# First norm of the next pair in the second feed-forward, value buffers cleared by ACT between its key copies, coupling behind the third tile

## The reference, cut to what matters

```
x = x + attn_a(layernorm(x))   # local attention, 16 heads of 16, blocks of 32 tokens, softmax
x = x + ffn(layernorm(x))      # three cycles of a gated coupling
x = x + attn_b(layernorm(x))   # differential attention, 32 half heads over all 1024 tokens
x = x + ffn(layernorm(x))
```

```
def layernorm(x):  return (x - mean(x)) / sqrt(var(x) + 1e-5)
def attn_a(x):     q, k, v = x @ w_qkv.T + b_qkv; softmax(q k / 4) v in blocks of 32 tokens
def ffn(x):
    gf = global_net(mean over tokens of x)
    out = x
    for _ in range(3):
        tf = sigmoid(gelu(gelu(gelu(out@w1+b1)@w2+b2)@w3+b3)@w4+b4)
        coupling = 0.1 + range * (0.7*gf + 0.3*tf - 0.5) * 2
        out = out + coupling * twist(out)      # twist permutes quarters of the features
    return out
```

## Time and profile before

| | us |
|---|---|
| median of 3 runs | 8516.29 |
| lowest, highest | 8493.72, 8532.59 |
| the profiled execution's own time | 8488.95 |
| its span (first to last instruction) | 8484.5 |
| PE, DVE, ACT, POOL busy | 7651.8, 6965.3, 6290.1, 3252.0 |
| mean granted clock of PE, share of full | 0.959 |

### The profile page before, as it was taken

How to read it: one execution, slowest core, us unless ns; L and a number is a source line. 1 busy time by engine, 2 the same in 40 slices (tenths; PEclk the granted TensorE clock), 3 DMA queues, 4 the chain that set the end, 5 groups by cost and what they waited for, 6 DMA issues and landing times. The chain is left out here.

```text
span 8484.5 us, 166411 instructions
## 1 busy us (share of the span) xinstructions
PE 7651.8 (90%) x65584; PEld 2773.6 (33%) x65584; DVE 6965.3 (82%) x8955; ACT 6290.1 (74%) x11674; POOL 3252.0 (38%) x4567
## 2 busy tenths in 40 slices
PE   6899978999789997899988999889998899979999
PEld 3322343223432234322343223432234322343223
DVE  5899768997689976899768997689976899668996
ACT  3699756997569975699756997569975699656996
POOL 3244232442324423344233442334423344234441
PEclk9999989999899998999999999999999999989999
DMA  0100001000010000100001000010000100001000
GB/s 30 46 21 23 17 11 46 21 24 15 11 46 21 24 15 11 46 24 21 15 11 46 25 21 15 11 50 21 22 19 6 50 21 25 18 4 50 22 23 21
DMA packets 219176, 205.43 MB, mean 24 GB/s; under 512 B 108086, under 2 KB 143414, under 8 KB 218358
## 3 DMA queue, kind: packets, MB, share of 16 engines
q1 hardware_dynamic: 218364, 194.46, 8.0%
HBM read 123.83 MB, written 67.37 MB: 23 GB/s over the span
## 5 line engine op out<-in xcount | busy, mean ns | idle before, releaser
L1440 DVE TENSOR_REDUCE mfull<-ps 128x1 f32<-128x1024 f32 x4096 | 4707.9, 1217 | 328.6 <-PE ps L1362 327.7
L1515 ACT ACTIVATE work<-ps 128x512 f32<-128x512 f32 x8192 | 4405.8, 598 | 373.6 <-PE ps L1384 257.5
L1402 PE MATMUL ps<-work,vbuf 128*32 128x256 f32 x32768 | 2624.1, 392 | 119.5 <-ACT hh L1535 119.5
L1362 PE MATMUL ps<-kop,qop 48*128 48x512 bf16 x8192 | 2490.4, 385 | 47.8 <-DVE mfull L1440 24.3
L1384 PE MATMUL ps<-qop,kop 51*128 51x512 bf16 x8192 | 2488.8, 384 | 0.9 <-DMA qop<-mT 0.7
L1402 PEld LDWEIGHTS ps<-work,vbuf 128*32 128x32 f32 x32768 | 654.4, 108 | 1769.3 <-issue 968.2
L1384 PEld LDWEIGHTS ps<-qop,kop 51*128 51x128 bf16 x8192 | 481.6, 93 | 1641.3 <-ACT work L1515 1525.8
L1466 POOL CAST mpart<-mfull 128x16 bf16<-128x16 f32 x256 | 50.4, 197 | 2467.0 <-issue 2004.2
L251 POOL TENSOR_TENSOR rstd<-rstd,nhalf 128x8 f32<-128x8 f32 x64 | 109.3, 1707 | 1632.4 <-DVE rstd L245 1632.4
L1484 POOL TENSOR_TENSOR work<-work,none 128x16 f32<-128x16 f32 x224 | 650.3, 2903 | 18.8 <-POOL mpart L1470 1.5
L450 POOL TENSOR_TENSOR hh<-work,hmask 128x1024 f32<-128x1024 f32 x256 | 520.7, 2062 | 111.4 <-PE ps L382 79.0
(11 more groups left out here) (178 smaller groups left out, 8868.0 us busy)
## 6 DMA issues: line engine op xcount, KB each, us to landing
qop<-scratch SPq DMA_DIRECT2D x512, 64.0 KB
scratch<-work SPq DMA_DIRECT2D x32, 768.0 KB, 4.1
scratch<-hh SPq DMA_DIRECT2D x32, 768.0 KB, 3.6
kop<-scratch SPq DMA_DIRECT2D x256, 96.0 KB
vbuf<-in_x SPq DMA_DIRECT2D x9, 2048.0 KB, 8.3
qop<-scratch SPq DMA_DIRECT2D x512, 32.0 KB
kop<-scratch SPq DMA_DIRECT2D x256, 64.0 KB
qop<-mT SPq DMA_DIRECT2D x1024, 3.0 KB
```

Source lines behind the costliest of these rows:

```text
L1362: pe.matmul(ps[:, b + n, :], qop[r:r + KQ, s, i, t * P:(t + 1) * P], kop[r:r + KQ, s, i, half(n)], start=True, stop=True).then_inc(s_ms, 1)
L1402: mm = pe.matmul(ps[VW * i:VW * (i + 1), OB, cols], vp[:, b, t, (G * gl + i) // 2, :], prob[:, u % PS, i, cols], start=t == 0 and part == ...
L1440: v.tensor_reduce(mfull[:, m // CUT % 2, r // ROWS * G // 2 + i, to:to + 1], ps[:, b:b + NB, :].rearrange("p b n -> p (b n)"), AX.X, ALU.m ...
L1515: act.activation(prob[:, u % PS, hl, :], ps[:, EB[slot % len(EB)], :], ACT.Exp, scale=scale).then_inc(s_ex, 1)
```

## The change

`first_pair` normalises, turns and keeps all 16 tiles instead of 8, and POOL clears `work[:, 8N:12N]` and `low` in that block. The block n1 is gone from the loop, and `layernorm` loses the arguments that served it. In f2 (`following`), behind the last residual tile, DVE normalises tiles 8 to 15 of the next pair into `h`; PE turns them behind the four key pieces, into banks 0 to 3, once two of these pieces are kept; and ACT and DVE keep them. ACT clears the four pieces of buffer by copying a broadcast column of zeros (a new tile `zero`), one of 2048 elements ahead of each key copy. In f2 alone, `couple(1, 2)` and `couple(1, 3)` stand ahead of tiles 3 and 4 of sequence 0.

```diff
@@ first_pair
-                    for t in range(T):
+                    for t in range(TT):
                         v.tensor_scalar(h[:, t, :], xin[:, t, :], mv[:, t, 0:1], rstd[:, t:t + 1],
                                         ALU.subtract, ALU.mult).then_inc(s_h, 1)
+                @block.gpsimd
+                def _(pool):
+                    pool.memset(work[:, 8 * N:12 * N], 0.0)
+                    pool.memset(low[:, :], 0.0)
+
                 @block.tensor
                 def _(pe):
-                    for t in range(T):
+                    for t in range(TT):
                         norm_turned(pe, t, s_h, s_tp)
-                    pe.wait_ge(s_ln, C * NB)
+                    pe.wait_ge(s_ln, C * CH)
                     for k in range(len(KV)):
                         first_keys(pe, k, 2 * k, s_qk)
                 @block.scalar
                 def _(act):
-                    for n in range(NB):
+                    for n in range(CH):
+                        b, cols = chunk_of(n)
                         act.wait_ge(s_tp, 4 * (n + 1))
                         for c in range(C):
-                            act.copy(hT[:, 0, c, half(n)], ps[:, c * NB + n, :]).then_inc(s_ln, 1)
+                            act.copy(hT[:, b, c, cols], ps[:, 4 * b + c * NB + n % NB, :]).then_inc(s_ln, 1)
@@ ffn, tensor
                             first_keys(pe, k, 2 * k, s_nqk)
+                        pe.wait_ge(s_nqke, 2)
+                        for t in range(T, TT):
+                            pe.wait_ge(s_nh, t + 1)
+                            for c in range(C):
+                                at = (t % 4) * P
+                                mm = pe.transpose(ps[:, c * NB + t % T // 4, at:at + P], h[:, t, c * P:(c + 1) * P],
+                                                  ident[:, :])
+                            mm.then_inc(s_ntp, 1)
@@ ffn, scalar
                     if following:
                         act.wait_ge(s_y, CH)
+                        act.wait_ge(s_pre, len(COUPLED))
+                        act.wait_ge(s_rw, 16 * len(COUPLED) // NB)
                         for k in range(len(KV)):
+                            clear = (work[:, 8 * N:10 * N], work[:, 10 * N:12 * N], low[:, 0:2 * N],
+                                     low[:, 2 * N:4 * N])[k]
+                            act.copy(clear, zero[:, 0:1].to_broadcast([P, 2 * N]))
                             act.wait_ge(s_nqk, k + 1)
                             keep_first_keys(act, k, 2 * k, s_nqke)
+                        for n in range(NB):
+                            act.wait_ge(s_ntp, T + 4 * (n + 1))
+                            act.copy(hT[:, 1, 0, half(n)], ps[:, n, :])
@@ ffn, vector
-                    for t in range(T):
-                        if t == T - 1:
-                            couple(1, 2)
-                        add_twisted(0, t)
-                    couple(1, 3)
+                    at = (T - 1, T) if q is None else (3, 4)
+                    for t in range(T + 1):
+                        if t in at:
+                            couple(1, 2 + at.index(t))
+                        if t < T:
+                            add_twisted(0, t)
...
+                    if following:
+                        v.wait_ge(s_xo, TT)
+                        v.wait_ge(norm[2], PB)
+                        for t in range(T, TT):
+                            v.tensor_scalar(h[:, t, :], xin[:, t, :], mv[:, t, 0:1], rstd[:, t:t + 1],
+                                            ALU.subtract, ALU.mult).then_inc(s_nh, 1)
+                        for n in range(NB):
+                            v.wait_ge(s_ntp, T + 4 * (n + 1))
+                            v.tensor_copy(hT[:, 1, 1, half(n)], ps[:, NB + n, :])
@@ the loop
-            layernorm("n1", x=xin, later=True)
             local_attention(n2)
```

More of the change, by code:

```diff
@@ L107, in build @@
         none = sb("none", [P, DH // 2])
+        zero = sb("zero", [P, 1])
         hb4 = sb("hb4", [P, 1])
@@ L168, in _ @@
                 pool.memset(none[:, :], -1.0).then_inc(s_c, 1)
-                pool.wait_ge(s_c, 2)
+                pool.memset(zero[:, :], 0.0).then_inc(s_c, 1)
+                pool.wait_ge(s_c, 3)
             s_v0, s_lam = sem("s_v0"), sem("s_lam")
@@ L227, in _ @@
                 pool.tensor_tensor(rstd[:, :], rstd[:, :], nhalf[:, :], ALU.pow).then_inc(s_c, 1)
-                pool.wait_ge(s_c, 3)
+                pool.wait_ge(s_c, 4)
             @block.sync
@@ L251, in root, with norm_turned @@
             pool.tensor_tensor(rstd[:, sequence], rstd[:, sequence], nhalf[:, sequence], ALU.pow).then_inc(s_rs, 1)
-        def norm_turned(pe, t, s_h, s_tp, seen=0):
-            pe.wait_ge(s_h, t + 1 - seen)
+        def norm_turned(pe, t, s_h, s_tp):
+            pe.wait_ge(s_h, t + 1)
             for c in range(C):
@@ L259, in norm_turned, with layernorm @@
             mm.then_inc(s_tp, 1)
-        def layernorm(tag, norm=None, x=x, ahead=None, later=False, stale=None):
+        def layernorm(tag, norm, ahead=None, stale=None):
             s_h, s_tp = ahead[0:2] if ahead else (sem(f"{tag}_{n}") for n in ("h", "tp"))
-            N0 = NB if ahead or later else 0
-            seen = 4 * NB if later else 0
+            N0 = NB if ahead else 0
             with nc.Block() as block:
@@ L280, in _ @@
                         v.sem_clear(stale)
-                    if norm:
-                        spread(v, norm, 1)
+                    spread(v, norm, 1)
                     for n in range(N0, CH + 1):
                         if n < CH:
-                            if norm and n % NB == 0:
+                            if n % NB == 0:
                                 v.wait_ge(norm[2], n // NB + 1)
@@ L292, in _ @@
                 def _(pool):
[L293 to L298, removed]
+                    root(pool, norm, 1)
                 @block.tensor
@@ L302, in _ @@
                     for t in range(4 * N0, TT):
-                        norm_turned(pe, t, s_h, s_tp, seen)
+                        norm_turned(pe, t, s_h, s_tp)
                 @block.scalar
@@ L308, in _ @@
                         b, cols = chunk_of(n)
-                        act.wait_ge(s_tp, 4 * (n + 1) - seen)
+                        act.wait_ge(s_tp, 4 * (n + 1))
                         act.copy(hT[:, b, 0, cols], ps[:, 4 * b + n % NB, :])
```

2 lines of the change are left out of this document (1 added, 1 removed).

## The result

The changed kernel takes 8449.58 us, the median of 4 runs (8440.70 to 8451.68), against 8516.07 for the kernel before (4 runs, 8493.72 to 8532.59). The ratio is 0.9922, its 95% interval 0.9898 to 0.9945: 66.5 us less, where the sum said 69.2 and the forecast 8447. The same kernel once more, beside other kernels, gave 8449.45 (ratio 0.9926, 0.9909 to 0.9942).

A forecast was written before the change was run, and what follows sets the result against it. No engine spans the kernel; the pair handover holds a stage of 11.34 us overlapping nothing after it. 7 x (11.34 - 1.56) = 68.5, +2.3 first pass, -1.6 last: 69.2 less, 8516.3 to 8447 us; range 8408 to 8486.

The forecast's parts named there:

- Removed, 11.34 us in each of seven passes: Loop's head: the stage that only normalises, turns and clears goes whole, saving 11.34 us in seven of eight passes.
- The base of the sum: Whole kernel: 69.2 us taken off the runs' median 8516.3 gives 8447; off the profiled 8488.95 it gives 8419.8.
- The signs of being wrong: Pair handover: wrong if key copies exceed 3.5 us apart, last copy to L450 exceeds 3, or pairs exceed 1046.
- Tail +1.56: End of second feed-forward: PE's 16 added turns and their copies lengthen the tail by 1.56 us in all eight passes.
- DVE's tiles hidden: Second feed-forward: eight added normalising tiles at 0.334 us each end at 1111.1, ahead of PE's 1112.32, so hidden.
- Clears at 2.0: Second feed-forward, ACT: each 2048-element clear takes 2.0 us and fits the key-copy gaps with 0.3 us to spare.
- Coupling at 0: Second feed-forward: moving the coupling behind the third tile gains 0.1 us, priced at 0; 3.3 us of cover left.
- First pair +9.0: First pair's block: 16 tiles beside POOL's two clears delay first keys by 9.0 us; that pass saves 2.3.
- the bound with the slow turns: First pair's block: PE's turns at 3.68 us for 16 put first keys at 51.4 instead of 42.14, +9.3 us.
- Rival B, a wait for instructions at the loop's head: Local attention behind the branch pays one more 1.6 us wait in seven passes, giving 8458 us; chance 0.08.
- Rival C, the clock: TensorE's clock settles the wrong way: five 1051.3 us pairs become like the slower ones, +26 us, 8473; chance 0.14.
- The clock's gain at nothing: PE at the handover: no clock gain taken; bounds 2.6 us gained a pass, or a slow stretch further on.

The follow-up runs named there:

- e1: The kernel before with only the clears moved to ACT (POOL in the first pair's block), the norm staying at the head; 8487.57 us, ratio 0.9956.
- e3: The changed kernel with each of ACT's four clears done twice; 8491.23 us, ratio 0.9961.
- e4: The changed kernel with the coupling back in its old order, around the eighth tile of the first sequence; 8455.27 us, ratio 0.9924.
- e2: The changed kernel with the clears given back to POOL, inside the second feed-forward behind the buffers' last use; 8454.98 us, ratio 0.9919.
- e6: The changed kernel with the local attention's first two value products put ahead of its first scores on PE; 8435.47 us, ratio 0.9917.
- e9: e6 plus POOL's first-pair clears put behind DVE's tiles; ACT still clears in f2, POOL at the fifth tile; 8429.51 us, ratio 0.9891.
- e7: e2 plus the fifth-tile clear moved into the feed-forward, and POOL's first-pair clears behind DVE's tiles; 8454.31 us, ratio 0.9937.
- e8: The changed kernel with the edits of e6 and e7 together; 8419.29 us, ratio 0.9901.
- e10: e8 run again in five rounds, nothing changed; 8421.23 us, ratio 0.9881.
- e11: e8 with all four value products of the first sequence, instead of two, ahead of the first scores; 8442.74 us, ratio 0.9911.
- e5: The changed kernel run again, unchanged, as the measure for other experiments; 8449.45 us, ratio 0.9926.

## Why the prediction was right, point by point

- **Removed, 11.34 us in each of seven passes.** Right: 13.34 us from the last key copy to the masked keys became 3.33, and e1 shows what the 11.34 were made of, 6.02 of clears and 5.32 of norm.
- **The base of the sum.** Right in part by luck. The sum was taken off the median of the runs (8447) and not off the profiled execution (8419.8), for the reason that this was the fastest of the four known. From profile to profile it missed: the changed kernel's is 8448.90 us, 29 above 8419.8. The forecast held because the median it started from is, by the estimate above, one of long passes already.
- **The signs of being wrong.** One of the three came up. The pairs are 1047.9 us apart and not under 1046, a bound that fits the short passes of before (1051.3 - 9.8 = 1041.5). The key copies stayed 3.43 us apart, and the way to the masked keys is 2.02.
- **Tail +1.56.** 1.31: PE's turns began 0.20 us ahead of the last key copy, where the sum had them beside it, and took 1.91 us instead of 1.97.
- **DVE's tiles hidden.** Right: 2.67 us for eight, ended at 1109.14, 1.1 ahead of PE's turns.
- **Clears at 2.0.** 1.89, with 0.53 us left in each gap instead of the 0.3 forecast; e3 shows the price without the gap. The estimate from the Trainium skill ("VectorE: DVE Perf Modes", the section on the TRN2 errata) was 1.89, and the trace agrees, also for a broadcast source.
- **Coupling at 0.** 0.08 us, and the median of e4 (8455.27) is that of e2 beside it (8454.98). The wait of 4.1 us was 4.03, and the cover left was 3.50 where 3.3 was said.
- **First pair +9.0.** +9.26 (51.40 against 42.14), by the bound with the slow turns (30 in 6.25 us). Why they are slower there than behind the keys (16 in 1.91) isn't shown; the profile has no low clock in that block. Two tiles wait, one for each clear, as the row with x2 and the idle of 2.91 show. e2 adds a sharper form: DVE's `tensor_scalar` is held, its three-operand residuals are not. It adds a limit too: one clear held one instruction here, but in one pass of e2 two clears in a row held the same one.
- **Rival B, a wait for instructions at the loop's head.** A late start came, but on ACT alone and off the path: ACT's table load starts 2.3 to 3.6 us behind POOL in the seven passes behind a branch, with nothing that the profile shows to wait for, and 0.03 us ahead of it in the first pass. The exponential behind it still waits 1.5 to 2.8 us for DVE. It is late, by 0.6 to 3.8 us, in every kernel that has ACT's clears and the local attention straight behind the branch (e3 to e6 and e9 as well). With the clears on POOL (e2, e7, e8, e10, e11) it starts 0.07 to 0.09 us ahead of POOL in all seven passes, and in e1, with ACT's clears but the short block n1 behind the branch, it comes 1.96 us behind the last key copy, as in the kernel before. So it goes with ACT's program on both sides of the branch; that it is a fetch of code isn't shown.
- **Rival C, the clock.** From profile to profile this is what happened: six of the seven passes measured are long, and 8419.8 + 26 = 8446 is near the profiled 8448.90. On the median it did not cost its 26 us (8473), since the runs of before, by the estimate above, had no short passes to lose. The step was framed on the one profiled execution, and no run shows the kinds of pass in the timed runs of before.
- **The clock's gain at nothing.** Right for the first value products, 6.25 against 6.32 us, although PE's idle did shrink to the 4.70 us forecast. Against the short passes of before the other bound came: a low stretch further on, 20 us behind the head.

## What to carry to other kernels

A stage that only prepares the next one can be worth nearly its whole length (here 11.34 us less a tail of 1.31) when every engine has a gap in the stage ahead; look there first for the gaps of the engine that already waits between its own copies. Ask of a memset beside a normalising tile who is held by whom: moving the memset alone was worth 39 us (e1), where the whole change and e2 are worth 66 to 72. And compare passes of the same kind before comparing two profiles: here the two profiles said 40 and the runs 66.

## What the runs showed that I had not expected

- ACT reads a broadcast column of one element into 2048 at 1.89 us, 0.92 ns an element, no dearer than the plain data of the earlier trace rows (1047 ns for 1024, 1.02 ns an element).
- A memset of 3.51 us on POOL leaves DVE's `scalar_tensor_tensor` on fp32 in SBUF alone (0.35 and 0.48 us) and holds even a `tensor_scalar` of 8 elements (0.82 instead of 0.17). Once in seven passes the latter stayed held through a second memset straight behind the first (4.28 us).
- ACT's first instruction behind the loop's branch can come up to 3.8 us late (e5) while POOL starts on time, or not late at all; it goes with ACT's programs ahead of and behind the branch; what decides it is open.
- With the same instructions, passes of one execution differ by 4 to 9 us. Whether PE's clock falls a second time some 20 us into the local attention moves the first regrouping by 4.6 to 4.9 us; a low stretch of 44 us some 260 us in goes with the longest pass.
